# One attention and two-level expert layer on one core: the masked phi(k) v product transposed in 32x32 blocks on VectorE

## The reference, cut to what matters

```python
x = inputs                                      # (16, 512, 256) float32
xn = layernorm(x)
# attention, 16 heads of 16: phi(u) = elu(u) + 1
q, k, v = phi(xn @ Wq + bq), phi(xn @ Wk + bk), xn @ Wv + bv
kv = einsum('bkhd,bkhm->bhdm', k, v)
att = einsum('bqhd,bhdm->bqhm', q, kv) / maximum(sum_k(q . k), 1e-6)
# feed-forward on all 8192 rows
shared = swiglu(xn @ w_in.T) @ w_out.T
group  = argmax(softmax(xn @ wg.T + gb))        # 2 groups of 4 experts
w_se   = top-2 probabilities within the group   # of 8 experts
routed = sum_e (swiglu(xn @ w1.T) * w_se[:, e]) @ w2[e].T
out = x + att @ Wo + bo + shared + routed
```

## Time and profile before

| | us |
|---|---|
| median of three runs | 980.45 |
| the profiled execution's own time | 985.9 |
| its span, first to last instruction | 983.9 |
| TensorE busy | 938.5 |
| VectorE busy | 679.5 |
| GpSimd busy | 475.0 |
| ScalarE busy | 364.6 |

### The profile page before, as it was taken

One profiled execution on the slowest core, in us unless ns is written; L12 is line 12 of the kernel. 1 busy time (PEld: TensorE's weight loads), 2 busy tenths in 40 slices (PEclk: granted clock), 3 DMA queues, 4 the chain that ended last, 5 costly groups with the idle time before them and its releaser, 6 DMA issues. The chain is left out here.

```text
span 983.9 us, 21262 instructions
## 1 busy us (share of the span) xinstructions
PE 938.5 (95%) x6302; PEld 845.0 (86%) x6303; DVE 679.5 (69%) x1723; ACT 364.6 (37%) x611; POOL 475.0 (48%) x529
## 2 busy tenths in 40 slices
PE   6899999999999999999999999999999999999993
PEld 5697989888897979898888979798989999999993
DVE  5959586776858595866768585958667766666662
ACT  4444534352534445343525344443432221222220
POOL 5736352634435363626344353536252555555555
PEclk9999999999999999999999999999999999999997
DMA  9130211111120302111111203021165777777760
GB/s 282 43 119 34 85 48 70 64 53 64 53 91 27 117 32 85 58 60 64 53 68 50 95 22 117 35 83 43 54 208 136 136 135 126 125 129 124 125 115 8
DMA packets 106262, 84.59 MB, mean 86 GB/s; under 512 B 23552, under 2 KB 97152, under 8 KB 106240
## 3 DMA queue, kind: packets, MB, share of 16 engines
q1 hardware_dynamic: 66384, 49.03, 16.7%
q0 software_dynamic: 17968, 25.32, 12.4%
q10 hardware_dynamic: 21888, 9.97, 3.8%
HBM read 45.57 MB, written 40.13 MB: 87 GB/s over the span
## 5 line engine op out<-in xcount | busy, mean ns | idle before, releaser
L325 PE MATMUL bank<-wexp_hi,xnT_hi 128*128 (+1 forms) x560 | 193.4, 345 | 14.0 <-issue 6.5
L327 PE MATMUL bank<-wexp_hi,xnT_lo 128*128 (+1 forms) x560 | 186.8, 334 | 0.0
L326 PE MATMUL bank<-wexp_lo,xnT_hi 128*128 (+1 forms) x560 | 186.4, 333 | 0.0
L1091 POOL TENSOR_TENSOR h_lo<-gated,h_hi 128x256 fp32r<-128x256 f32 x128 | 99.7, 800 | 108.8 <-ACT h_hi L641 108.8
L1114 POOL TENSOR_TENSOR res<-res,bvo 128x256 f32<-128x256 f32 x64 | 52.8, 853 | 204.7 <-DMA res<-x 204.7
L325 PEld LDWEIGHTS bank<-wexp_hi,xnT_hi 128*128 128x128 f32 x560 | 106.6, 190 | 33.6 <-issue 24.2
L327 PEld LDWEIGHTS bank<-wexp_hi,xnT_lo 128*128 128x128 f32 x560 | 106.5, 190 | 11.0
L326 PEld LDWEIGHTS bank<-wexp_lo,xnT_hi 128*128 128x128 f32 x560 | 106.8, 191 | 9.4
L325 PE MATMUL bank<-xnT_hi,win_hi 128*128 128x512 f32 x256 | 101.2, 395 | 0.1
L327 PE MATMUL bank<-xnT_hi,win_lo 128*128 128x512 f32 x256 | 99.9, 390 | 0.0
L326 PE MATMUL bank<-xnT_lo,win_hi 128*128 128x512 f32 x256 | 99.8, 390 | 0.0
(11 more groups left out here) (185 smaller groups left out, 2472.1 us busy)
## 6 DMA issues: line engine op xcount, KB each, us to landing
xt<-x SPq DMA_DIRECT2D x16, 512.0 KB, 3.5
res<-x SPq DMA_DIRECT2D x16, 512.0 KB, 3.6
out<-res SPq DMA_DIRECT2D x16, 512.0 KB, 2.9
xt<-h_d SPq DMA_DIRECT2D x76, 64.0 KB
xt<-h_d ACTq DMA_DIRECT2D x76, 64.0 KB
kb<-h_d SPq DMA_DIRECT2D x76, 64.0 KB
kb<-h_d ACTq DMA_DIRECT2D x76, 64.0 KB
wstage<-w_exp SPq DMA_DIRECT2D x16, 256.0 KB, 3.6
```

What stands on the lines that cost most here:

```text
L325: e.matmul(to, w_hi, m_hi_, start=first_, stop=False, skip_group_check=free)
L326: e.matmul(to, w_hi, m_lo_, start=False, stop=False, skip_group_check=free)
L327: return e.matmul(to, w_lo, m_hi_, start=False, stop=last_, skip_group_check=free)
L1091: ins = pool.tensor_tensor(h_lo[:, j, cols], gated[:, j % 2, cols], h_hi[:, j, cols].bitcast(f32), ALU.subtract)
```

## The change

1. The two TensorE transposes of `kvm` and ScalarE's copy go, with their semaphore `kvt_done`. VectorE transposes `kvm` in 32x32 blocks to `kvT`, right after `gate(b, 1, 1)`. As `kvm` is zero outside the 16x16 blocks of the diagonal, this is the whole transpose.
2. TensorE's waits for `sil_rdy` and `rsil_rdy` before products go; those for the gates, which come after them, stay.
3. `routed_gate(b, 0, 4)` moves into `table_rows`, ahead of its last four instructions, and `routed_gate(b, 1, 1)` ahead of the reciprocal chain.
4. TensorE's register loads move from the group's start to the middle of the first and the fifth tile, each for the next half group; `info_i` is laid out so that one load fetches both experts of four tiles, and takes two casts.
5. GpSimd's staging instructions are cut in pieces of 256 columns.
6. In the expert stage, GpSimd's `entries` come after the second and the sixth scatter of a group.

```diff
-        info_i = sb("info_i", [1, 3, NT], i32)
+        info_i = sb("info_i", [1, 3 * NT], i32)
+        experts_i = info_i[:, 0:2 * NT].rearrange("p (t n) -> p t n", n=2)
+        at_i = info_i[:, 2 * NT:3 * NT]
...
+        def rows_of(engine, first, n):
+
+            return nc.values_load_multi_w_load_instructions(at_i[:, bass.ds(first, n)], [engine], min_val=0, max_val=SENT,
...
-                pe.wait_ge(kvm_rdy, b + 1)
-                for c in range(DC):
-                    mm = pe.transpose(bank[2][:, c * P:(c + 1) * P], kvm[:, c, :], ident)
-                mm.then_inc(kvt_done, 1)
-
-                pe.wait_ge(sil_rdy, HC * b + 2)
                 pe.wait_ge(gate_rdy, HC * b + 2)
                 routed(1, (0, 1))
 
-                pe.wait_ge(rsil_rdy, TB * b + 1)
                 pe.wait_ge(rg_rdy, TB * b + 1)
...
-                pe.wait_ge(rsil_rdy, TB * b + 2)
                 pe.wait_ge(rg_rdy, TB * b + 2)
...
+            expert_regs = [nc.alloc_registers(f"expert{n}", [mybir.EngineType.PE]) for n in range(2 * GT)]
+
+            def experts_in(q, half):
+
+                nc.regs_load(expert_regs[2 * TB * half:2 * TB * (half + 1)],
+                             experts_i[:, bass.ds(q * TB, TB), :].rearrange("p t n -> p (t n)"))
+
             def group(g, last):
                 tiles = LAST_TILES if last else GT
 
-                experts = [register_row(mybir.EngineType.PE, n, g * GT, tiles, (E - 1) * HC * D) for n in range(2)]
                 for t in range(tiles):
-                    at = experts[0][t], experts[1][t]
+                    at = [nc.snap(r, [mybir.EngineType.PE], min_val=0, max_val=(E - 1) * HC * D)
+                          for r in expert_regs[2 * t:2 * t + 2]]
                     wait(pe, ysum, GT * g + t - 7)
...
                             mm = mm3(pe, bank[t][:, n * D:(n + 1) * D], rh_hi[t % TB][:, j, :], rh_lo[t % TB][:, j, :],
                                      wexp_hi[:, bass.ds(off, D)], wexp_lo[:, bass.ds(off, D)],
                                      n == 0 and j == 0, j == HC - 1, True)
+                        if n == 0 and t % TB == 0 and not last:
+                            experts_in(2 * g + t // TB + 1, 1 - t // TB)
                     mm.then_inc(sw_done, 1)
 
+            experts_in(0, 0)
...
                 routed_silu(b, 0, 3)
-                act.wait_ge(kvt_done, b + 1)
-                act.copy(kvT[:, :, :].rearrange("p c n -> p (c n)"), bank[2][:, 0:DC * P]).then_inc(kvT_rdy, 1)
                 routed_silu(b, 1, 0)
...
                 link(dve.tensor_tensor(cmq[:, :, :, :], cmp[:, :, :, :], wi, ALU.mult))
+                routed_gate(b, 0, 4)
                 dve.tensor_copy(pos_i[:, :], pos[:, :])
                 dve.tensor_copy(rows[:, :, 0], tok[:, :])
                 link(dve.tensor_reduce(wts[:, :, 2], q, AX, ALU.add))
...
                 gate(b, 1, 1)
+                dve.wait_ge(kvm_rdy, b + 1)
+                dve.transpose(kvT.rearrange("p c n -> p (c n)"), kvm.rearrange("p c n -> p (c n)")).then_inc(kvT_rdy, 1)
                 ranks_in(b)
...
                 table_rows(b)
-                routed_gate(b, 0, 4)
+                routed_gate(b, 1, 1)
 
...
                                   own_block.unsqueeze(2).broadcast_to([P, TB, P]), ALU.mult).then_inc(rn_rdy, 1)
-                routed_gate(b, 1, 1)
                 if last:
...
-                    dve.tensor_copy(info_i[:, :, :].rearrange("p n t -> p (n t)"), bank[5][0:1, 0:3 * NT]).then_inc(infoi_rdy, 1)
+                    dve.tensor_copy(experts_i.rearrange("p t n -> p n t"), bank[5][0:1, 0:2 * NT].rearrange("p (n t) -> p n t", n=2))
+                    dve.tensor_copy(at_i, bank[5][0:1, 2 * NT:3 * NT]).then_inc(infoi_rdy, 1)
...
+            def low_part(buf, hi, lo, done):
+                for b_, h_, l_ in zip(cut_in(buf, 4), cut_in(hi, 4), cut_in(lo, 4)):
+                    ins = pool.tensor_tensor(l_, b_, h_.bitcast(f32), ALU.subtract)
+                ins.then_inc(done, 1)
+
+            def high_part(buf, hi):
+                for b_, h_ in zip(cut_in(buf, 4), cut_in(hi, 4)):
+                    ins = pool.tensor_copy(h_, b_)
+                ins.then_inc(pool_set, 1)
...
-                pool.tensor_tensor(lo, buf, hi.bitcast(f32), ALU.subtract).then_inc(ffn_split, 1)
+                low_part(buf, hi, lo, ffn_split)
             pool.wait_ge(w1_ld, 16 * 2)
             pool.wait_ge(w_round, len(stage_kv) + len(stage_q) + len(stage_in) + 1)
-            pool.tensor_tensor(stage_w1[0][3], stage_w1[0][0], stage_w1[0][2].bitcast(f32), ALU.subtract).then_inc(w1_split, 1)
...
+            low_part(stage_w1[0][0], stage_w1[0][2], stage_w1[0][3], w1_split)
+            high_part(stage_w1[1][0], stage_w1[1][2])
+            pool.wait_ge(pool_set, 3)
+            low_part(stage_w1[1][0], stage_w1[1][2], stage_w1[1][3], w1_split)
+            pool.wait_ge(out_w_ld, 16 * 3)
+            wout_hi_, wout_lo_ = (w[:, :, :].rearrange("p c n -> p (c n)") for w in (wout_hi, wout_lo))
+            high_part(wstage[:, :], wout_hi_)
+            pool.wait_ge(pool_set, 4)
+            low_part(wstage[:, :], wout_hi_, wout_lo_, ffn_split)
...
+            def scatter(g, t):
+                if t % TB == 0:
+                    wait_apart(pool, idxc_rdy, 2 * g + t // TB + 1)
+                wait_apart(pool, ysum, GT * g + t + 1)
+                pool.indirect_dma_start(out, bass.IndirectOffsetOnAxis(ap=idx_cur[:, t // TB, t % TB:t % TB + 1], axis=0), ring[t], None,
+                                        bounds_check=N - 1, oob_is_err=False, compute_op=ALU.add).then_inc(out_st[t], 16)
 
             def group(g, last):
-                if last:
-                    scatter(g, 0, LAST_TILES)
-                else:
-                    entries(g, 1)
-                    scatter(g, 0)
-                    entries(g + 1, 0)
-                    scatter(g, 1)
+                for t in range(LAST_TILES if last else GT):
+                    scatter(g, t)
+                    if not last and t == 1:
+                        entries(g, 1)
+                    if not last and t == 5:
+                        entries(g + 1, 0)
```

More of the change, by code:

```diff
@@ L277, in wait_apart @@
                 e.sem_inc(passed, 1)
-        def register_row(engine, row, first, n, most):
-            return nc.values_load_multi_w_load_instructions(info_i[0:1, row, bass.ds(first, n)], [engine], min_val=0, max_val=most,
+        def rows_of(engine, first, n):
+            return nc.values_load_multi_w_load_instructions(at_i[:, bass.ds(first, n)], [engine], min_val=0, max_val=SENT,
                                                             skip_runtime_bounds_check_because="tile_list sums one slot or none for each tile")[1]
@@ L447, in batch @@
                     if t == 0:
-                        wait(pe, rsil_rdy, TB * b)
                         wait(pe, rg_rdy, TB * b)
@@ L543, in batch @@
                     mm.then_inc(nb_done, 1)
-                pe.wait_ge(rsil_rdy, TB * b + 3)
                 pe.wait_ge(rg_rdy, TB * b + 3)
@@ L556, in batch @@
                     mm.then_inc(info_done, 1)
-                pe.wait_ge(rsil_rdy, TB * (b + 1))
                 pe.wait_ge(rg_rdy, TB * (b + 1))
@@ L731, in _ @@
             act.wait_ge(t_done, DC * B)
[L732 removed]
+            rows_at = rows_of(mybir.EngineType.Activation, 0, TB)
             for t in range(2):
@@ L1136, in _, with cut_in @@
             reciprocal_root(0)
+            def cut_in(of, n):
+                return [of[:, k * 256:(k + 1) * 256] for k in range(n)]
+            def low_part(buf, hi, lo, done):
[6 more added lines that the diff above has]
+                ins.then_inc(pool_set, 1)
             for n, (buf, _, hi, lo) in enumerate(stage_in):
                 pool.wait_ge(w_round, len(stage_kv) + len(stage_q) + n + 1)
[L1139 removed]
+                low_part(buf, hi, lo, ffn_split)
             pool.wait_ge(w1_ld, 16 * 2)
             pool.wait_ge(w_round, len(stage_kv) + len(stage_q) + len(stage_in) + 1)
[L1142 to L1148 removed]
+            low_part(stage_w1[0][0], stage_w1[0][2], stage_w1[0][3], w1_split)
[7 more added lines that the diff above has]
+            low_part(wstage[:, :], wout_hi_, wout_lo_, ffn_split)
             rounds(pool, batch, B)
@@ L1158, in entries @@
                 pool.tensor_copy(idx_cur[:, half, :], cur[:, half, :, 0]).then_inc(idxc_rdy, 1)
-            def scatter(g, half, tiles=TB):
-                wait_apart(pool, idxc_rdy, 2 * g + half + 1)
-                for t in range(TB * half, TB * half + tiles):
-                    wait_apart(pool, ysum, GT * g + t + 1)
-                    pool.indirect_dma_start(out, bass.IndirectOffsetOnAxis(ap=idx_cur[:, half, t % TB:t % TB + 1], axis=0), ring[t], None,
-                                            bounds_check=N - 1, oob_is_err=False, compute_op=ALU.add).then_inc(out_st[t], 16)
-            def group(g, last):
-                if last:
```

(11 more changed lines are left out.)

12 lines of the change are left out of this document (2 added, 10 removed).

## The result

The changed kernel takes 969.05 us (median of four runs, 968.47 to 971.81); the kernel before, on the same chip, 981.1 (977.77 to 982.82). The ratio is 0.9887, with a 95% interval of 0.9854 to 0.992. It is faster, as forecast, and 1.8 us above the predicted 967.3. The medians are 12.05 us apart.

The account below looks back on a forecast made before the run. TensorE, busy 95% of the span, was taken as the bound. Terms -3.5 + 6.0 + 0.5 - 9.4 - 6.8 = -13.2 us, subtracted from the median 980.45, gave 967.3 us; range 952 to 977.

Parts of the forecast that it names:

- batch 0: Staging in 256-column pieces lets VectorE in between, cutting TensorE's waits and half-clock time: -3.5 us, ends 0 and -5.
- handover: Before SyncE's first load for the expert stage, the transpose and two `info` casts instead of one: +0.5 us.
- nine groups: Expert stage: interleaving removes the scatter waits, TensorE sets the pace, 23.2 us a group: 208.8 against 218.2, -9.4 us.
- end: Last scatter starts 0.3 us after VectorE's last sum rather than 7.1: -6.8 us, ends -3 and -7.
- transposes' own gain of 0: Removing TensorE's transposes, 0.44 us a batch, gives 0: `gate(b, 1, 1)` fixes `routed(1)`, some 0.3 us idle becomes visible.
- batch term: VectorE's transpose pushes small products into GpSimd's subtraction, `routed_gate(b, 0, 4)` 0.4 us later: +6.0 us in 15 batches.
- if neither does, 0.8 later: Hand count: if neither small product passes ahead of GpSimd's pieces, `routed_gate(b, 0, 4)` starts 0.8 us later.
- one passes: Hand count: if the first small product passes with the copy of `run`, the gate starts 0.2 us later; 0.4 was taken.
- Rival 1: VectorE's copy of `run` or products slip between GpSimd's pieces; batch term -6.8, 954.5 us; chance 0.25.
- Rival 2: SyncE's loads bound the expert stage at 24 us a group; sum -4.2, 976.3 us; chance 0.13.
- rival 3: Interleaving has no effect, a copy still waits out a scatter each half; 983.5 us, no change; chance 0.06.
- Rival 4: TensorE, idle twice a batch, loses clock in 15 batches; +22.5 us, 989.8 us, slower; chance 0.04.

Follow-up runs that it names:

- experiment 3: The changed kernel with kvm transposed on TensorE and copied on ScalarE as before, gates still early: 961.04 us, ratio 0.977 to the kernel before.
- experiment 5: The changed kernel with VectorE's transpose moved behind the table rows, ahead of `routed_gate(b, 1, 1)`: 958.67 us, ratio 0.9763 to the kernel before.
- experiment 9: The kernel before with only its transpose moved to VectorE, behind `gate(b, 1, 1)`: 996.93 us against 982.49, ratio 1.0131.
- experiment 4: The changed kernel with GpSimd's second subtraction, `low(1)`, moved behind the four table scatters: 962.27 us, ratio 0.9785 to the kernel before.
- experiment 11: The changed kernel run again with nothing edited: 969.72 us, ratio 0.9863 to the kernel before.
- experiment 2: The changed kernel with the old order of scatters and table copies put back: 986.38 us, ratio 1.0015 to the kernel before.
- experiment 7: The changed kernel with TensorE's two register loads put back at each group's start: 972.04 us, ratio 0.9895 to the kernel before.
- experiment 1: The kernel before with only the new order of scatters and GpSimd's table copies: 972.39 us against 984.76, ratio 0.9888.

## Why the prediction was right, and where its terms were off

| term | forecast | measured | from |
|---|---|---|---|
| batch 0 | -3.5 (0 to -5) | +0.25 | `routed(2)` of batch 1 at 87.28, before 87.03 |
| batches 1 to 15 | +6.0 (-6.8 to +12) | +3.8 | the same of batch 15: 721.31, before 717.23 |
| handover | +0.5 (0 to +1) | +0.2 | from there to tile 1: 26.66, before 26.43 |
| nine groups | -9.4 (-11 to -2) | -11.9 | tile 1 to the last product: 211.92, before 223.80 |
| end | -6.8 (-3 to -7) | -6.3 | last product to the span's end: 10.1, before 16.4 |
| sum | -13.2 | -13.9 | spans 970.0 and 983.9 |

The table cuts at tile 1, the second of the stage, because TensorE's wait moved from the front of tile 0 (1.25 us) to the front of tile 1 (1.00). From the first product of the first group to that of the tenth, as the prediction counted, it is 207.5 us against 218.2: -10.7, where 208.8 and -9.4 were forecast.

*The transposes' own gain of 0.* Right: experiments 3 (with them, 44.51 us a batch) and 5 (without, 44.55) are alike. The 0.44 us of products were replaced by 0.2 to 0.4 us of waiting for the gate ("some 0.3 us" was forecast).

*The batch term.* The mechanism was right: the transpose pushes the two products under GpSimd's subtraction, both rows are over 0.5 us, and `routed(2)` starts 0.23 later after the gate, at the low side of the 0.3 to 0.4 named. The size was off in the hand count: "if neither does, 0.8 later" was wrong. Neither passed, and the gate starts 0.30 later. By the starts of the rows, as in experiment 9, the gate leaves 0.91 us behind, and 0.32 + 0.56 + 0.44 - 0.10 come to it: +0.31. The step had let a product wait out a whole piece of 0.78 (two of them, less the 0.55 gained, would even be 1.0, not 0.8); in fact the two are held up by 0.55 and 0.43. That the 0.4 taken for "one passes" came so near the 0.26 a batch of "neither passes" is luck. Experiments 3, 4 and 5 take away the transpose, the subtraction and the meeting of the two, and each shortens a batch to 44.5 to 44.6 us. This was also the choice between the two pages. The rule of the Trainium skill (SBUF — State Buffer, "Who interferes with whom") that decided the term is borne out (0.72 us for 0.29 when the subtraction is first, 0.29 when the product is first by 0.02 us). The other rule of the Trainium skill (VectorE: DVE Perf Modes, "Rules for kernel authors"), that for a transpose within 32x32 blocks VectorE's is fastest, says nothing of the instructions behind it. The prediction had drawn its -6.8 from it; the operation is short, 0.44 us, and experiment 9 is still 1.3% slower.

*Rival 1, slipping through,* did not happen here, but it is what experiments 3 and 5 make happen, and they measure 961.04 and 958.67. Its batch term of -6.8 is what experiment 5 shows (630.5 to 623.7 in 14 periods). The 954.5 that the rival gave was too low by 4 to 7 us, and it was wrong to let it turn on luck: in all 16 batches of the changed kernel the product is blocked (703 to 733 ns), and in 14 of the 16 of experiment 5 it isn't: the order is set by the program, not by chance.

*Batch 0* failed as a step. "VectorE then gets in between" holds only where GpSimd has pauses. The forecast didn't ask when `w_out` lands. The two `phiq` sums do shorten, from 4.03 us to 2.38 in the first profile, but they begin at 31.38 instead of 29.79, as the chain of small products ahead of them is now held up. The start of batch 1's normaliser's products, 82.58 before, is at 82.61 there and at 81.06 in experiment 11; in experiments 2 and 7, which have the same batches, it is at 80.84 and 83.92. So it is anything from -1.7 to +1.3, not -3.5.

*The groups* were mis-sized the other way. The prediction took 23.2 us from the first four groups of before as TensorE's own pace, with the register loads hidden "as in the first groups" and "behind a full queue" costing nothing. Only the first three ran at that pace, 23.06 in the mean; the fourth, 24.72, was already slow. The groups measure 22.84 now, and experiment 7 shows where the difference lies: the loads cost 0.33 us a group even behind a full queue. The waits for scatters were the main part, as said: experiment 1 gets 10 us out of the stage with that edit alone. Rival 2, the loads of rows, is refuted by the groups of 22.84 us, and rival 3 by copies of `cur` that wait for no scatter; experiment 2 makes what rival 3 described, 986.38, no change.

*The end* was right, 0.5 us too large: the last scatter begins 0.78 us after VectorE's last sum (960.82 + 0.48), where it was 7.1.

*Rival 4, the clock.* TensorE stands still twice a batch, 0.36 and 0.61 us in batch 7, and keeps its clock. Experiment 9, with 0.46 and 1.08 us, does so too. So the rival's forecast is refuted, but its "idle time between 1.25 us and 2.75" doesn't hold either: in batch 0 of experiment 3 the clock fell after single waits of 1.04, 0.29 and 0.40 us (0.58 granted from 35.2 to 38.6). The window from 300 to 700 us of experiment 9 (columns as in the earlier trace rows):

```profile
300.00:700.00 400.00, 386.29 (x2408) 337.35 (x2407) 290.06 (x783) 170.99 (x284) 180.96 (x221) 1.00 0.18 62
```

The range and the sign held, but errors that offset each other made the sum look better than its terms: batch 0 came out 3.7 us too high, the batches and the groups together 4.7 too low. That is luck. The median was missed by 1.8 us on the other side because the terms come from profiled executions, which are 13.9 us apart, while the medians are 12.05 apart.

## What to carry to other kernels

A bundle of edits can be faster while the edit that names it is slower; here the scatters' order alone brought as much as the whole, the gates moved up were worth another 0.52 us a batch, and the transpose where it was put took that back and more (8 to 12 us between the changed kernel and experiments 3 and 5). Before moving an operation to VectorE ahead of small dependent operations, look at what GpSimd starts next: 0.36 us of work cost 0.81 a batch because it changed who came first, and the same work put behind the table rows cost nothing that shows (44.55 us a batch against 44.51 without it). Where GpSimd issues scatters and must see them landed before it may overwrite their indices, put other scatters between the issue and the wait. And once a stage runs at another engine's pace, a shorter TensorE gives nothing there: its 1.0 to 1.1 us of register loads at a dry group's start were idle time that GpSimd's 24.8 us a group had in any case.

## What the runs showed of the hardware

- VectorE operations with a single input can be held up by GpSimd as well. The cast of four columns of `pos` to int32 took 604 ns in the median of 16 batches of the kernel before, where it falls into the subtraction, and 170 in experiment 9, where it does not. The 128x32 copy of `run` took 182 in the median of experiment 9 and once 702. The 128x256 transpose was not held up: it took 0.44 us beside a running subtraction (355.13, GpSimd from 354.07 to 355.59) as it did in experiment 5 where GpSimd stood still (350.63). The gate, with one operand in PSUM, took 0.69 beside the same subtraction. The Trainium skill (SBUF — State Buffer, "Who interferes with whom") lists casts and copies among those that can take the shared pair of ports, and the cast agrees.
- Which side loses such a meeting was decided by 0.02 us in batch 7 of experiment 5, the same way in 14 of 16 batches, and for `rank<-rank,oh` it is 0.43 us of VectorE's chain.
- The first 40 us of identical programs differ by 2.8 us between two executions (35.80 and 33.04), one in which GpSimd did not have to pause for a weight transfer and one in which it paused 3.49 us; a profile of one execution can't tell the value of an edit there.
- After 2.43 us and 1.13 us of idleness in batch 0 the granted clock was 0.57 for 3.5 us; after 0.63 and 0.62 in experiment 11 it stayed 1.00, and after 1.08 in batch 7 of experiment 9 too. The length of the waits alone doesn't tell: after 0.84 and 1.13 us in batch 0 of experiment 4 the clock fell to the lower level, 1.2 GHz (0.50 from 36 to 38 us), and after 0.75 and 1.14 in that of experiment 5 it stayed at the upper one. The windows of the two, experiment 4 first (columns as in the earlier trace rows); at the lower level ten products fall into the 3 us in place of fourteen:

```profile
36.00:39.00 3.00, 3.00 (x10) 2.33 (x9) 2.90 (x9) 0.00 (x0) 2.92 (x6) 0.57 0.00 0
```

```profile
36.00:39.00 3.00, 3.00 (x14) 2.38 (x14) 2.90 (x9) 1.04 (x3) 2.92 (x6) 1.00 0.00 0
```
